# Feed-forward stage: scaled product kept in PSUM (three banks), maxima over pairs of chunks, ScalarE's taps two chunks ahead

## The reference, cut to what matters

```
h  = bit_linear(layernorm(x), w1)      # 512 -> 2048 channels
h  = conv_w[:,0]*h[t-1] + conv_w[:,1]*h[t] + conv_w[:,2]*h[t+1] + conv_b    # depthwise, zeros at both ends
h  = silu(h)
x += bit_linear(h, w2)                 # 2048 -> 512
bit_linear(x, w): x is rounded to whole numbers in -127..127 of its row's largest absolute value,
                  w is rounded to -1, 0 or 1 of its mean absolute value, then x @ w.T, scaled back
```

## Time and profile before

| | us |
|---|---|
| median of three runs | 3311.36 (3308.74 to 3317.6) |
| profiled execution, its own time | 3314.49 |
| its span, first to last instruction | 3312.7 |
| feed-forward stage within it | about 590 to 1164 |

### The profile page before, as it was taken

One profiled execution on the slowest core, in us unless ns is written; L12 is line 12 of the kernel. 1 busy time (PEld: TensorE's weight loads), 2 busy tenths in 40 slices (PEclk: granted clock), 3 DMA queues, 4 the chain that ended last, 5 costly groups with the idle time before them and its releaser, 6 DMA issues. The chain is left out here.

```text
span 3312.7 us, 44462 instructions
## 1 busy us (share of the span) xinstructions
PE 2574.8 (78%) x14146; PEld 1327.2 (40%) x14147; DVE 1853.1 (56%) x2672; ACT 1203.9 (36%) x1807; POOL 910.4 (27%) x741
## 2 busy tenths in 40 slices
PE   8377777356666658888887509999999999999970
PEld 4244444122232234444444204444444444444430
DVE  4477776789889676676664642223233333332225
ACT  2233333287887655555554421111111111111110
POOL 0010100066776711111111170005055311350017
PEclk9788888678888879999998859999999999999995
DMA  9560000100000020000000361003033211220018
GB/s 217 119 238 8 7 8 5 51 0 1 1 0 0 0 63 9 9 8 8 11 8 14 117 225 42 32 32 108 32 108 103 76 62 50 89 95 32 32 52 274
DMA packets 118043, 194.11 MB, mean 59 GB/s; under 512 B 55264, under 2 KB 55264, under 8 KB 117456
## 3 DMA queue, kind: packets, MB, share of 16 engines
q1 hardware_dynamic: 92607, 102.96, 11.4%
q0 software_dynamic: 25360, 90.21, 8.0%
HBM read 122.65 MB, written 70.48 MB: 58 GB/s over the span
## 5 line engine op out<-in xcount | busy, mean ns | idle before, releaser
L1806 PE MATMUL e_gate_up<-weights,e_x_t 128*128 x3456 | 772.2, 380 | 1.4 <-ACT e_x_t L1860 1.4
L1806 PEld LDWEIGHTS e_gate_up<-weights,e_x_t 128*128 128x128 bf16 x3456 | 332.8, 98 | 377.4 <-issue 5.1
L1893 DVE TENSOR_TENSOR e_mid<-e_gate,e_gate_up 128x512 f32<-128x512 f32 x144 | 98.9, 687 | 645.8 <-ACT e_gate L1866 645.8
L1826 PE MATMUL e_out<-weights,e_mid_t 128*128 x1728 | 384.7, 379 | 1.1 <-DVE e_mid_t L1906 1.1
L1866 ACT ACTIVATE e_gate<-e_gate_up 128x512 f32<-128x512 f32 x144 | 86.0, 597 | 684.6 <-PE e_gate_up L1806 684.6
L559 PE MATMUL a_turn<-a_wo,a_mixed_t 128*128 128x512 bf16 (+1 forms) x1024 | 284.9, 435 | 2.4 <-DVE a_mixed_t L817 1.7
L1826 PEld LDWEIGHTS e_out<-weights,e_mid_t 128*128 128x128 bf16 x1728 | 169.0, 98 | 204.8 <-issue 1.2
L492 POOL TENSOR_TENSOR a_probs<-a_e,a_probs 128x616 bf16<-128x616 f32 x64 | 85.6, 1353 | 516.4 <-ACT a_probs L726 516.4
L1015 POOL TENSOR_TENSOR f_shared<-f_shared 128x512 f32<-128x512 f32 x128 | 181.0, 1415 | 124.4 <-DVE f_shared L1293 124.4
L1085 PE MATMUL f_out<-f_w,hidden 128*128 128x512 f16 x512 | 143.7, 409 | 91.2 <-ACT hidden L1187 90.7
L650 ACT ACTIVATE a_probs_t<-a_flip 77x512 f32<-77x512 f32 (+1 forms) x256 | 192.3, 801 | 53.7 <-PE a_flip L508 53.6
(11 more groups left out here) (239 smaller groups left out, 4279.8 us busy)
## 6 DMA issues: line engine op xcount, KB each, us to landing
raw_weights<-in_w POOLq DMA_DIRECT2D x72, 512.0 KB, 4.0
sorted_x<-a_zero_row POOLq DMA_DIRECT2D x1, 18432.0 KB, 55.9
e_x_rows<-sorted_x SPq DMA_DIRECT2D x72, 256.0 KB, 2.7
sorted_y<-e_y_rows SPq DMA_DIRECT2D x72, 256.0 KB, 2.0
raw_weights<-in_w SPq DMA_DIRECT2D x24, 512.0 KB, 4.0
x<-in_x SPq DMA_DIRECT2D x4, 2048.0 KB, 21.7
out<-x SPq DMA_DIRECT2D x32, 256.0 KB, 4.1
hidden<-in_w_t SPq DMA_DIRECT2D x1, 4096.0 KB, 14.4
```

Source lines behind the costliest of these rows:

```text
L1806: last = nc.tensor.matmul(gate_up[half][:, part, :], x_t[:, u, a, k, :], plan.weights13[:, bass.ds(expert % 2, 1), b, k, col:col + 512], s ...
L1826: last = nc.tensor.matmul(out[:, :], mid_t[:, a, j, :], plan.weights2[:, bass.ds(expert % 2, 1), b, j, :], start=(j == 0 and a == b == 0), ...
L1893: nc.vector.tensor_tensor(mid[:, half, :], gate[:, half, :], gate_up[half][:, 1, :], ALU.mult).then_inc(mid_made, 1)
```

## The change

- The scaled product is written back to its own PSUM bank. There are three banks (`bank_of`: j % 3, and bank 1 for chunk 15), `padded` and its two waits are gone, and both the taps and the left tap read the bank. The left and right taps cover 511 tokens in place of padding. `first` now waits for the left tap of the bank's last user (`since`: 3 chunks back as a rule, 4 for chunks 0 and 2, 2 for chunks 1 and 15).
- For the third bank, `front` shares the bank `scales_bank`. So the first `flip` of a batch waits for `row_copied`, and the flips move from steps 8 and 11 to 9 and 12.
- The maxima are taken over 8 pairs of chunks, seven of them inside the loop (at step 3, 5, ... 15), the last after it.
- ScalarE's step j becomes `silu(j-1)`, `round_up(j)`, `taps(j+2)`, where it was `taps(j+1)`, `round_up(j)`, `silu(j-1)`.
- VectorE's step j does the left tap before `scale_down(j+2)`, where it was after.

```diff
     BUF = 4
-    GROUPS = ((0, 5), (5, 10), (10, 14), (14, HC))
+    GROUPS = tuple((lo, lo + 2) for lo in range(0, HC, 2))
...
         down_row = sb("down_row", [P, 2, S])
-        padded = sb("padded", [P, BUF, S + 2])
...
         up2_row = sb("up2_row", [P, S])
-        product = [pb(f"product{i}", [P, 512]) for i in range(2)]
+        product = [pb(f"product{i}", [P, 512]) for i in range(3)]
         out = [pb(f"out{i}", [P, 512]) for i in range(TPS)]
-        front = pb("front", [P, 2, 512], F16)
-
         scales_bank = pb("scales_bank", [P, 512])
+        front = scales_bank[:, :].bitcast(F16).rearrange("p (i n) -> p i n", i=2)
+        bank_of = [*(j % 3 for j in range(HC - 1)), 1]
+        turns = bank_of * 2
+        since = [next(d for d in range(1, HC) if turns[HC + j - d] == turns[HC + j]) for j in range(HC)]
...
                         pool.wait_ge(left_added, HC * b + j + 1)
-                        nc.gpsimd.tensor_tensor(y[:, j % BUF, :], y[:, j % BUF, :], side[:, j % BUF, :], ALU.add
-                                                ).then_inc(right_added, 1)
+                        nc.gpsimd.tensor_tensor(y[:, j % BUF, 0:S - 1], y[:, j % BUF, 0:S - 1],
+                                                side[:, j % BUF, 0:S - 1], ALU.add).then_inc(right_added, 1)
...
             def flip(n, pair):
                 pe.wait_ge(rounding, TPS * n + 2 * pair + 2)
+                if pair == 0:
+                    pe.wait_ge(row_copied, n + 1)
...
                 flip(0, pair)
-            pe.wait_ge(row_copied, 1)
+            pe.wait_ge(front_copied, TPS // 2)
...
             last.then_inc(columns_ready, 1)
-            pe.wait_ge(front_copied, TPS // 2)
             def first(b, j, parity):
-                at_least(pe, scaled_down, HC * b + j - 1)
+                at_least(pe, left_added, HC * b + j - since[j % HC] + 1)
                 for k in range(KD):
-                    last = nc.tensor.matmul(product[j % 2][:, :], w1[:, k, j % HC * P:(j % HC + 1) * P],
+                    last = nc.tensor.matmul(product[bank_of[j % HC]][:, :], w1[:, k, j % HC * P:(j % HC + 1) * P],
...
                         scales_row(b + 1)
-                    if has_front and j in (8, 11):
-                        flip(b + 1, j // 11)
+                    if has_front and j in (9, 12):
+                        flip(b + 1, j // 12)
...
                     pe.wait_ge(tops_made, b + 1)
-                    at_least(pe, row_copied, b + 1 + has_front)
+                    pe.wait_ge(front_copied, TPS // 2 * (b + 1 + has_front))
...
                 at_least(act, hidden_made, HC * b + j + 1 - BUF)
-                nc.scalar.activation(y[:, j % BUF, :], padded[:, j % BUF, 1:S + 1], ACT.Identity,
+                scaled = product[bank_of[j % HC]]
+                nc.scalar.activation(y[:, j % BUF, :], scaled[:, :], ACT.Identity,
                                      bias=column(conv_b, j % HC), scale=conv_w[:, j % HC, 1:2])
-                nc.scalar.activation(side[:, j % BUF, :], padded[:, j % BUF, 2:S + 2], ACT.Copy,
+                nc.scalar.activation(side[:, j % BUF, 0:S - 1], scaled[:, 1:S], ACT.Copy,
...
             taps(0, 0)
+            taps(0, 1)
...
                     for j in range(HC):
-                        if j + 1 < HC or has_front:
-                            taps(b, j + 1)
-                        round_up(j)
...
                             silu(j - 1)
+                        round_up(j)
+                        if j + 2 < HC or has_front:
+                            taps(b, j + 2)
...
             ternary(1, w2_in, w2)
-            dve.wait_ge(zeroed, 8)
+            dve.wait_ge(small_in, 32)
             def scale_down(b, j, parity):
                 dve.wait_ge(product_ready, HC * b + j + 1)
-                at_least(dve, taps_made, HC * b + j + 1 - BUF)
-                at_least(dve, left_added, HC * b + j + 1 - BUF)
-                nc.vector.tensor_tensor(padded[:, j % BUF, 1:S + 1], product[j % 2][:, :], down_row[:, parity, :],
-                                        ALU.mult).then_inc(scaled_down, 1)
+                bank = product[bank_of[j % HC]]
+                nc.vector.tensor_tensor(bank[:, :], bank[:, :], down_row[:, parity, :], ALU.mult
+                                        ).then_inc(scaled_down, 1)
...
                 for j in range(HC):
+                    if has_middle:
+                        dve.wait_ge(taps_made, HC * b + j + 1)
+                        nc.vector.scalar_tensor_tensor(y[:, j % BUF, 1:S], product[bank_of[j]][:, 0:S - 1],
+                                                       conv_w[:, j, 0:1], y[:, j % BUF, 1:S], ALU.mult, ALU.add
+                                                       ).then_inc(left_added, 1)
...
                         scale_down(b, j + 2, 1 - parity)
-                    if has_middle:
-                        dve.wait_ge(taps_made, HC * b + j + 1)
-                        nc.vector.scalar_tensor_tensor(y[:, j % BUF, :], padded[:, j % BUF, 0:S],
-                                                       conv_w[:, j, 0:1], y[:, j % BUF, :], ALU.mult, ALU.add
-                                                       ).then_inc(left_added, 1)
-                    for g in range(len(GROUPS) - 2):
-                        if has_middle and j == GROUPS[g][1] + 2:
+                    for g in range(len(GROUPS) - 1):
+                        if has_middle and j == GROUPS[g][1] + 1:
...
                 if has_middle:
-                    largest(len(GROUPS) - 2)
```

More of the change, by code:

```diff
@@ L997, in _ @@
             nc.gpsimd.memset(minus[:, :], -OFFSET / P).then_inc(zeroed, 1)
-            nc.gpsimd.memset(padded[:, :, 0:1], 0.0).then_inc(zeroed, 1)
-            nc.gpsimd.memset(padded[:, :, S + 1:S + 2], 0.0).then_inc(zeroed, 1)
             def iteration(b, parity, has_middle, has_back, has_front):
```

## The result

Over 20 runs each, the changed kernel takes 3318.07 us (3312.05 to 3326.71), the kernel before 3310.35 (3304.32 to 3317.6): ratio 1.0024, interval 1.0017 to 1.0031, so it is slower, by some 7.7 us. The median forecast was 3314. The profiled span grew from 3312.7 to 3320.1 us.

A forecast was written before the change was run, and what follows sets the result against it. Middle iterations were taken as bound by ScalarE's queue plus the turn. Iteration 0 -4.4, 1 +0.3, 2 to 6 +10.8, 7 -4.5 sum to +2.2: 3316.7 us own time, 3314 median; range 3303 to 3325, 8 in 10 3294 to 3331.

The forecast's parts named there:

- the turn: ScalarE's standstill from an iteration's last silu to up2_row; forecast to go from 9.65 to 7.35 us.
- (f): Full steps: the loop silu, round_up, second takes 2.41 us against ScalarE's 2.37; 0.4 lost, 0.5 more at steps 12 and 15.
- (a): After up2_row, ScalarE's round_up(0) waits for scale_up(0): 1.5 us lost.
- (g): Full steps with TensorE at its low clock: matmuls take longer, 1.2 us for one such step (0 to 3.6).
- (c): silu(0) waits for second(0), which stands behind first(3) waiting for left(0): 1.0 us (0 to 2.1).
- (e): Step 9's flip waits for copy_row, second(8) stands behind it and silu(8) waits for that: 1.7 us lost.
- (b): taps(2) waits for scale_down(2), which stands on VectorE behind the adds and left(0): 2.2 us lost.
- (d): VectorE's scales come behind largest(0), which waits for silu(1), so taps(6) is late by 1.2 us (0 to 2).
- rest: Remaining effects cost nothing: memsets, starting waits, no DMA, and bank 1's short distance at chunks 15 and 17 is covered.
- Rival A: Faster: (c), (d), (f) and (g) come to nothing; -24 us, 3287; chance 0.25 with the ground towards it.
- rival B: Slower: full steps of iterations 1 to 6 loop through second at the low clock; +27 us, 3338; chance 0.22.
- C: Rival: scaling in place in PSUM is dear for VectorE, 1.2 us per scale_down; +8 on the forecast, 3322; chance 0.09.

The follow-up runs named there:

- e1: Changed kernel with copy_row one step earlier on ScalarE (step 7 in place of 8); ratio 0.9966 to the kernel before.
- e6: Changed kernel with second(0) ahead of first(3) on TensorE, nothing else; ratio 0.9992 to the kernel before.
- e7: Changed kernel with the four normed rows in step 0, two ahead of round_up(0), two behind it; ratio 1.0025 to the kernel before.
- e3: Kernel before with only the maxima over pairs (seven in the loop, the last after it); ratio 0.9986 to the kernel before.
- e2: Changed kernel with ScalarE's old order (taps one chunk ahead), banks and maxima as changed; ratio 0.9939 to the kernel before.

## Why the prediction was right, and where it was off

The sum was +2.2, measured +7.4 in the profiled runs, within the stated range. It came out so because errors of either sign partly cancel: iterations 0 and 7 gave 1.8 where 8.9 were forecast, the five middle ones cost 7.9 where 10.8 were, and 0.9 lies outside the nine iterations. By its steps:

- *Iteration as ScalarE's queue plus the turn*: right as a picture. It gave 64.05 for a middle iteration and 61.2 for iteration 1; they are 63.5 and 61.3. The closeness is in part luck: over iterations 2 to 6 ScalarE's work, with the 0.4 of (f), is 48.2 where the sum had 47.4, and the listed waits are 7.8 where it had 9.3. The prediction's figures for the kernel before have the same two errors: 49.5, not 48.2, with stalls of 2.8 and not 3.9.
- *The turn*: 7.35 forecast, 7.4 idle measured.
- *(a) to (g)* in iteration 4: 1.5, 2.2, 1.0, 1.2, 1.7, 0.9, 1.2 forecast; 1.4, 2.6, 0.7, 0.7, 2.6 measured, and 0.4 at step 15 of (f). No wait of (g) stands by itself; (c) and (e) swing between 0.7 and 2.1 and between 1.7 and 2.6, and where they are long a product at the low clock stands before them (silu(8): 1.7 behind one of 1.03, 2.6 behind one of 1.77), so (g) is counted inside them. e1 and e6 show (e) and (c) by taking them away. The worth of (a) and (b) was mis-sized: each was an idle, but in e7, which takes (a) and half of (b) away, iterations 1 to 6 gain only 1.6 us in all while (c) stands behind them.
- *Iteration 0*, -4.4: it is -2.1, and the turn alone gave 2.2. That VectorE's lighter queue would end its last maximum at 697.6 failed; it ended at 701.1, of which 1.1 is the later start. ScalarE, TensorE and ScalarE again:

```profile
668.43 0.78 ACT L1172 ACTIVATE f_shared<-f_product,f_conv_b,f_conv_w 128x512 f32<-128x512 f32 x1 [2.31 <-DVE f_product L1265]
...
694.54 1.89 PE L1067 MATMUL f_product<-f_xq_t,f_w 128*128 128x512 bf16 x4 [1.95 <-DVE f_shared L1291]
...
697.19 0.78 ACT L1172 ACTIVATE f_shared<-f_product,f_conv_b,f_conv_w 128x512 f32<-128x512 f32 x1 [1.46 <-DVE f_product L1265]
```

Scales behind largest(0) cost 2.3, as in (d), a wait that iteration 0 of the kernel before does not have. Near the end first for chunk 17 waits for left(15), both on bank 1, and runs at the low clock, and the tap waits 1.5: the prediction's *rest* held that short distance covered. e3, without the banks, has iteration 0 at 53.6.
- *Iteration 7*, -4.5, is the step that failed: +0.3. It allowed for a slow step or so, and left out a longer wait of first. Its end, VectorE, TensorE, ScalarE:

```profile
1119.36 1.55 DVE L1286 TENSOR_TENSOR f_tops<-f_tops 128x512 f32<-128x512 f32 x1
1120.95 0.75 DVE L1291 SCALAR_TENSOR_TENSOR f_shared<-f_product,f_conv_w,f_shared 128x511 f32<-128x511 f32 x1
...
1122.21 0.74 DVE L1291 SCALAR_TENSOR_TENSOR f_shared<-f_product,f_conv_w,f_shared 128x511 f32<-128x511 f32 x1
...
1123.01 1.44 PE L1067 MATMUL f_product<-f_xq_t,f_w 128*128 128x512 bf16 x4 [2.29 <-DVE f_shared L1291]
...
1124.25 1.06 PE L1088 MATMUL f_out<-f_w,hidden 128*128 128x512 f16 x2
...
1126.26 0.63 ACT L1187 ACTIVATE hidden<-f_shared 128x512 f32<-128x512 f32 x1 [2.56 <-PE f_out L1088]
...
1131.96 0.63 ACT L1187 ACTIVATE hidden<-f_shared 128x512 f32<-128x512 f32 x1 [2.03 <-PE f_out L1088]
...
1135.24 0.63 ACT L1187 ACTIVATE hidden<-f_shared 128x512 f32<-128x512 f32 x1 [2.04 <-PE f_out L1088]
```

The full steps do run in 2.43 us, as the loop (f) of 2.41 says, until first for chunk 15 waits 2.3 us, the granted clock falls (0.96 from 1118 to 1124, 0.64 from 1124 to 1136), and three silus wait 2.6, 2.0 and 2.0 for a product at up to 1.91. Two things make that wait. The slowed maxima (1.55 for 0.69) push the left taps back; but they did so in earlier groups too (1.57 at 1113.98, where first waits 1.05 and the clock stays up). And chunk 15 is on bank 1, whose last user is chunk 13 and not 12: first stands behind the left tap at 1122.21, where one of the usual distance would stand behind that at 1120.95, 1.3 us earlier (an estimate from these rows; no run moves chunk 15 to another bank). Measured against the full step of 2.43, those three come 3.0, 0.8 and 0.8 us late, and an earlier tap pair 0.5: 5.1 of the 5.2 between 53 and 58.2. I had (g) in the list and allowed for one such step there, and I had bank 1's short distance in (f) at a fraction of a microsecond. e2, where a tap pair stands between round_up and silu, has this iteration at 53.0, though its first waits 3.0 us for the same left tap.
- *Left tap and PSUM*: 0.74 forecast, 747 ns. The Trainium skill, VectorE: DVE Perf Modes, section on the TRN2 errata, would have had 65 ns more for the PSUM source, an estimate from that page. The traces do not bear it out: the fastest left tap takes 737 ns from SBUF before and 737 from PSUM now. The taps gained 0.08 a chunk, as forecast, by the full steps of e2 and of the kernel before.

Rival A's ground was not entered: (c), (d), (e) all stand in the trace. Of rival B the mechanism is there, but at the end of iteration 7 and not in the full steps of iterations 1 to 6, which keep 2.43. C is out: scale_down costs 10 ns more. Of the signs, the first up2_row (706.3 for 703) and the last gap (58.2 for 53) failed, and GpSimd's scale_up is at 1.33, not 1.27; the middle gap, the left tap and the waits of ScalarE came as said.

## What to carry to other kernels

A buffer is freed by its last reader. Here the bank was to live until VectorE's left tap, a later reader, had read it. That turned VectorE's delays into waits of TensorE, and it paid only when VectorE's longest instruction was cut too. Count the distance between two users of a bank for every chunk: the one chunk with two in place of three stood before the longest waits of iteration 7. Before reordering an engine's queue, write down for each of its instructions which product it waits for and what stands ahead of that product on its own engine: two of the costs here, silu(8) behind a flip behind a copy and silu(0) behind a left tap, could be read off the code, and one line each took them away. An idle ahead of an arrival that is set elsewhere is worth little until the arrival is moved (e7).

## What the runs showed of the hardware

VectorE's maxima of two SBUF tensors (line 1286) take 0.69 us at the turn and up to 1.84 in the loop: 1.55 at 1119.36, for instance, beside GpSimd's instructions at 1119.10 and 1120.33. Its left tap takes 0.74 to 1.77 with two SBUF tensors (before) and 0.74 to 0.75 with one of them in PSUM (after), whatever GpSimd does. Four 512-column matmuls take 1.03 at 2.4 GHz and 1.91 at 1.2, and in the changed kernel the low level returned after first had waited 2.3 us in iteration 7, just where the loop through second had no slack for it.
